# Mirrored tiles of groups 5 and 6 of a graph-attention layer: transposed on TensorE instead of VectorE and DMA, and multiplied in their own step

## The reference

```
h    = relu(layernorm(x)) @ weight                     # 4096 x 256
hn   = h / norm(h)                                     # rows of length 1
P    = exp(hn @ hn.T) * (adj + 1e-8)                   # softmax of sim + log(adj + EPS), before the division
out  = (P @ h) / rowsum(P) + bias
x    = x + out
```

## Time and profile before

| | |
|---|---|
| time, median of 3 runs | 1313.46 us (1306.77 to 1319.57) |
| the profiled execution's own time | 1324.26 us |
| its span | 1322.5 us |
| granted TensorE clock, mean | 0.997 |
| PE busy | 1265.3 us (96%) |
| DVE busy | 986.2 us (75%) |
| ACT busy | 674.7 us (51%) |
| POOL busy | 348.5 us (26%) |

### The profile page before, as it was taken

The page is one execution under the profiler, slowest core; times in us unless marked ns, Lnnn a source line. Parts: engine busy times, 40 slices in busy tenths (PEclk is TensorE's granted clock), DMA queues, the critical chain, the costliest instruction groups (busy, mean ns, idle before and its releaser), DMA issues.

```text
span 1322.5 us, 26821 instructions
## 1 busy us (share of the span) xinstructions
PE 1265.3 (96%) x9548; PEld 942.2 (71%) x9548; DVE 986.2 (75%) x2264; ACT 674.7 (51%) x1504; POOL 348.5 (26%) x423
## 2 busy tenths in 40 slices
PE   6999989988999999989999999999999988989998
PEld 4788878863455555557777777777777766878887
DVE  7968777899555555569899978988989998674352
ACT  6664535555322223256565755766757654635421
POOL 2000000012423222222323322333332322354443
PEclk9999999999999999999999999999999999999999
DMA  9999999951121221025663553553646323351400
GB/s 230 282 291 336 327 325 327 370 216 60 57 65 49 64 65 32 17 64 169 188 186 112 168 176 122 173 174 111 189 133 178 116 96 105 96 160 39 130 26 25
DMA packets 122900, 199.95 MB, mean 151 GB/s; under 512 B 13200, under 2 KB 83856, under 8 KB 122768
## 3 DMA queue, kind: packets, MB, share of 16 engines
q1 hardware_dynamic: 115568, 194.04, 48.0%
q10 hardware_dynamic: 7200, 4.20, 1.1%
HBM read 147.85 MB, written 50.33 MB: 150 GB/s over the span
## 4 chain that ended last, share of the span: by engine, by line
PE 58%; DVE 13%; issue 8%; DMA 5%; POOL 4%; ACT 2%; SPq 1%; ACTq 1%; DVEq 0%; POOLq 0%
PE ps L1797 11%; PE ps L1684 8%; PE ps L1685 8%; PE ps L1782 7%; PE ps L1783 7%; PE ps L1892 7%; DMA acc<-in_adj 5%; DVE ring L834 4%; PE ps L1814 4%; PE ps L1853 3%; DVE small L846 2%; POOL ring L732 1%; SPq L469 1%; POOL w_all L755 1%; ACTq L485 1%
## 5 line engine op out<-in xcount | busy, mean ns | idle before, releaser
L732 POOL TENSOR_TENSOR ring<-ring 128x512 f16<-128x512 f32 (+2 forms) x133 | 148.7, 1119 | 354.0 <-ACT ring L1532 347.0
L1646 PE MATMUL ps<-val_hi,ring 128*128 128x257 f16 x1024 | 227.4, 274 | 8.4 <-DVE ring L834 8.4
L1647 PE MATMUL ps<-val_lo,ring 128*128 128x256 f16 x1024 | 227.3, 274 | 0.0
L1684 PE MATMUL ps<-ring,acc 128*128 128x512 fp8e4 x512 | 195.1, 381 | 8.5 <-DVE acc L972 8.5
L1797 PE MATMUL ps<-hnt 128*128 128x512 f16 (+3 forms) x864 | 196.3, 363 | 0.0
L1685 PE MATMUL ps<-ring,acc 128*128 128x512 fp8e4 x512 | 195.0, 381 | 0.0
L834 DVE STREAM_TRANSPOSE ring<-acc 128x1024 uint8<-128x1024 uint8 x128 | 151.0, 1218 | 40.3 <-DMA acc<-in_adj 40.2
L1411 ACT ACTIVATE hnt<-ring 128x512 bf16<-128x512 uint8 (+1 forms) x192 | 115.1, 602 | 88.1 <-DVE ring L834 88.1
L1782 PE MATMUL ps<-val_hi,hs 128*128 128x257 f16 x534 | 145.8, 273 | 0.4 <-DVE acc L1145 0.3
L1814 PE MATMUL ps<-val_hi,hs 128*128 128x257 f16 x534 | 145.8, 273 | 0.0
L1783 PE MATMUL ps<-val_lo,hs 128*128 128x256 f16 x534 | 145.6, 273 | 0.0
(11 more groups left out here) (234 smaller groups left out, 2384.0 us busy)
## 6 DMA issues: line engine op xcount, KB each, us to landing
acc<-in_adj SPq DMA_DIRECT2D x256, 256.0 KB, 9.1
turned_dram<-ring SPq DMA_DIRECT2D x56, 512.0 KB, 2.9
ring<-turned_dram SPq DMA_DIRECT2D x224, 128.0 KB, 2.9
at_dram<-ring SPq DMA_DIRECT2D x32, 512.0 KB, 10.1
ring<-at_dram SPq DMA_DIRECT2D x64, 256.0 KB, 4.0
ring<-at_dram SPq DMA_DIRECT2D x24, 512.0 KB, 3.9
ring<-at_dram SPq DMA_DIRECT2D x9, 1024.0 KB, 9.8
xs<-in_x SPq DMA_DIRECT2D x12, 256.0 KB, 10.5
```

What stands on the lines that cost most here:

```text
L732: nc.gpsimd.tensor_tensor(lo2[m % 2][:, k:GW], p2t[m % 2][:, k:GW], hi2[m % 2][:, k:GW], ALU.subtract).then_inc(sem["lo2_done"], 1)
L1646: nc.tensor.matmul(ps[:, k % 8, 0:D + 1], lhs, val_hi0[:, t, 0:D + 1], start=(t == 0), stop=False)
L1647: last = nc.tensor.matmul(ps[:, k % 8, 0:D], lhs, val_lo0[:, t, :], start=False, stop=(t == NB - 1))
L1684: nc.tensor.matmul(ps[:, bank + c, :], g_hi[:, t, c * P:(c + 1) * P], src, start=(t == 0), stop=False)
```

## The change

Outer steps of groups 5 and 6 become **near**, those of groups 0 to 4 stay **far**. For a near step the transpose on DVE, the write to DRAM and the read back are gone. PE transposes its four blocks into bank 6 (as for inner steps), DVE masks them in one operation of 128 x 512 out of bank 6, and the mirrored product comes in the step itself and not four steps later. The mirrored product of inner steps of groups 5 and 6 also moves from one step later to the step itself. Near products all go to bank 7, and so do far products at steps in which bank 6 holds transposes. The counts waited for are renumbered (`rank` is the place among outer steps in the order of the mirrored products; `flipped` is inner or near).

```diff
@@ -308,12 +308,17 @@
         n_outer = [sum(outer[:n]) for n in range(NS + 1)]
         n_inner = [sum(inner[:n]) for n in range(NS + 1)]
         LAG = 4
+        NEAR = 5
+        near = [outer[n] and order[n][0] >= NEAR for n in range(NS)]
+        far = [outer[n] and not near[n] for n in range(NS)]
+        flipped = [inner[n] or near[n] for n in range(NS)]
+        n_flipped = [sum(flipped[:n]) for n in range(NS + 1)]
 
         def mirrors_at(n):
 
 
-            return ([n - LAG] if 0 <= n - LAG < NS and outer[n - LAG] else []) + \
-                [o for o in (n - 1, n) if 0 <= o < NS and inner[o] and o + (order[o][0] < NG - 1) == n]
+            return ([n - LAG] if 0 <= n - LAG < NS and far[n - LAG] else []) + \
+                [o for o in (n - 1, n) if 0 <= o < NS and flipped[o] and o + (order[o][0] < NEAR) == n]
 
         mirror_order = [o for n in range(NS + LAG) for o in mirrors_at(n)]
         place = {o: m for m, o in enumerate(mirror_order)}
@@ -326,7 +331,7 @@
             for n in range(NS):
                 if outer[n]:
                     at = n + LAG
-                    free = at > 20 and not any(inner[o] and o - 1 <= at <= o for o in range(NS))
+                    free = far[n] and at > 20 and not any(flipped[o] and o - 1 <= at <= o for o in range(NS))
                     past = banks[n] = 6 if free and past == 7 else 7
             return banks
 
@@ -339,7 +344,14 @@
         def sums_in(bank, n):
 
 
-            return max([n_outer[o] + 1 for o in range(n) if outer[o] and mirror_bank(o) == bank] + [0])
+            return max([rank[o] + 1 for o in rank if rank[o] < rank[n] and mirror_bank(o) == bank] + [0])
+
+        rank = {o: i for i, o in enumerate(o for o in mirror_order if outer[o])}
+
+        def sums_before(n):
+
+
+            return max([rank[o] + 1 for o in rank if far[o] and o + LAG < n - 1 and mirror_bank(o) == 6] + [0])
 
         def first_block(n):
 
@@ -364,7 +376,7 @@
 
         def mirrored_last(g, b):
 
-            return any(inner[n] and order[n] == (g, g * GB + b) and n + (g < NG - 1) >= last_step(g, b) for n in range(NS))
+            return any(inner[n] and order[n] == (g, g * GB + b) and n + (g < NEAR) >= last_step(g, b) for n in range(NS))
 
         def last_step(g, b):
 
@@ -578,7 +590,7 @@
 
             sp.wait_ge(sem["z_piece"], piece_count(7, 3))
             load_raw(sp, 0, "11")
-            outer_steps = [n for n in range(NS) if outer[n]]
+            outer_steps = [n for n in range(NS) if far[n]]
             chunk_at = {last_in(c - 3) + 2: c for c in range(3, len(pairs))}
             mirror_chunk_at = {last_of(c - 3) + LAG + 1: c for c in range(3, len(mirror_pairs))}
             for n in range(NS):
@@ -1102,7 +1114,7 @@
                 m, r, b0 = place[n], order[n][1] % GB, mirror_blocks(n)[0]
                 since(dve, sem["lo2_done"], m - 1)
                 out = p2t[m % 2][:, b0 * P:GW]
-                if outer[n]:
+                if far[n]:
                     c, o = mirror_chunk_of(n), n_outer[n]
                     if r == 0:
                         dve.wait_ge(c2_loaded[c % 3], 16 * (c // 3 + 1))
@@ -1113,10 +1125,19 @@
                                                               chunk2[c % 3][:, q, r * P:(r + 1) * P].rearrange("p (a j) -> p a j", a=4),
                                                               EDGE * ATTN_EPS, came[:, o % 2, q], ALU.add, ALU.mult)
                     last.then_inc(sem["p2_done"], 1)
+                elif near[n]:
+                    c = mirror_chunk_of(n)
+                    if r == 0:
+                        dve.wait_ge(c2_loaded[c % 3], 16 * (c // 3 + 1))
+                    dve.wait_ge(sem["t_done"], n_flipped[n] + 1)
+                    nc.vector.scalar_tensor_tensor(out.rearrange("p (b i) -> p b i", i=P),
+                                                   chunk2[c % 3][:, :, r * P:(r + 1) * P], EDGE * ATTN_EPS,
+                                                   ps[:, 6, :].rearrange("p (b i) -> p b i", i=P),
+                                                   ALU.add, ALU.mult).then_inc(sem["p2_done"], 1)
                 else:
                     c = chunk_of(n)
                     dve.wait_ge(c1_loaded[c % 3], 16 * (c // 3 + 1))
-                    dve.wait_ge(sem["t_done"], n_inner[n] + 1)
+                    dve.wait_ge(sem["t_done"], n_flipped[n] + 1)
                     nc.vector.scalar_tensor_tensor(out.rearrange("p (b i) -> p b i", i=P),
                                                    chunk1[c % 3][:, b0:GB, r * P:(r + 1) * P], EDGE * ATTN_EPS,
                                                    ps[:, 6, b0 * P:GW].rearrange("p (b i) -> p b i", i=P),
@@ -1124,12 +1145,12 @@
 
             def add_mirror(n):
 
-                (g, j), m = order[n], n_outer[n]
+                g, j = order[n]
                 dve.wait_ge(sem["pv2_done"], place[n] + 1)
                 if g == 0:
                     nc.vector.tensor_copy(acc[:, j, :], ps[:, mirror_bank(n), 0:D + 1]).then_inc(sem["acc_added"], 1)
                 else:
-                    dve.wait_ge(sem["acc_added"], m - NB + (g + 1) * GB)
+                    dve.wait_ge(sem["acc_added"], rank[order.index((g - 1, j))] + 1)
                     nc.vector.tensor_tensor(acc[:, j, :], acc[:, j, :], ps[:, mirror_bank(n), 0:D + 1], ALU.add).then_inc(sem["acc_added"], 1)
 
             def group_sum(g, b):
@@ -1141,7 +1162,7 @@
                 if g == 0:
                     nc.vector.tensor_copy(acc[:, k, :], ps[:, b, 0:D + 1]).then_inc(sem["group_out"], 1)
                 else:
-                    dve.wait_ge(sem["acc_added"], n_outer[opens[g]])
+                    dve.wait_ge(sem["acc_added"], max(rank[o] + 1 for o in rank if o < opens[g]))
                     nc.vector.tensor_tensor(acc[:, k, :], acc[:, k, :], ps[:, b, 0:D + 1], ALU.add).then_inc(sem["group_out"], 1)
 
             def group_tail(g, i):
@@ -1310,7 +1331,7 @@
             for n in range(NS):
                 if n + 1 < NS:
                     weights(n + 1)
-                if n + 1 < NS and outer[n + 1]:
+                if n + 1 < NS and far[n + 1]:
                     turn(n + 1)
                 for o in mirrors_at(n - 1):
                     if outer[o]:
@@ -1335,14 +1356,14 @@
                     residual2(late_at["project1"][n])
                 if n + 1 < NS:
                     for o in mirrors_at(n + 1):
-                        if n + 1 in opens and outer[o]:
+                        if n + 1 in opens and far[o]:
                             mirror_weights(o)
                 if n + 1 in opens:
                     for b in range(GB):
                         group_sum(order[n][0], b)
                 if n + 1 < NS:
                     for o in mirrors_at(n + 1):
-                        if n + 1 not in opens or inner[o]:
+                        if n + 1 not in opens or flipped[o]:
                             mirror_weights(o)
                 if n in PREP:
                     prepare(n)
@@ -1511,10 +1532,10 @@
                 k = first_block(n) * P
                 nc.scalar.activation(ps[:, 4 + n % 2, k:GW], ps[:, 4 + n % 2, k:GW], ACT.Exp, scale=1.0 / VSC ** 2).then_inc(sem["exp_raw"], 1)
                 if n >= 2:
-                    if outer[n - 2]:
+                    if far[n - 2]:
                         act.wait_ge(sem["turned"], n_outer[n - 2] + 1)
-                    if inner[n - 2]:
-                        act.wait_ge(sem["t_done"], n_inner[n - 2] + 1)
+                    if flipped[n - 2]:
+                        act.wait_ge(sem["t_done"], n_flipped[n - 2] + 1)
                 act.wait_ge(sem["exp_raw"], n + 1)
                 nc.scalar.activation(e_t[n % 2][:, k:GW], ps[:, 4 + n % 2, k:GW], ACT.Copy, scale=PSC).then_inc(sem["exp_done"], 1)
 
@@ -1827,9 +1848,9 @@
             def mirror(n):
 
                 pe.wait_ge(sem["exp_done"], n + 1)
-                if n_inner[n] > 0:
-                    pe.wait_ge(sem["p2_done"], place[[o for o in range(n) if inner[o]][-1]] + 1)
-                since(pe, sem["acc_added"], sums_in(6, n - 1 - LAG))
+                if n_flipped[n] > 0:
+                    pe.wait_ge(sem["p2_done"], place[[o for o in range(n) if flipped[o]][-1]] + 1)
+                since(pe, sem["acc_added"], sums_before(n))
                 for b in mirror_blocks(n):
                     last = nc.tensor.transpose(ps[:, 6, b * P:(b + 1) * P], e_t[n % 2][:, b * P:(b + 1) * P], ident_f[:, :])
                 last.then_inc(sem["t_done"], 1)
@@ -1843,7 +1864,7 @@
                     if bank == 6:
                         for done in ("relu1", "ht2_low", "val2_ready", "hnt_ready"):
                             pe.wait_ge(sem[done], NB)
-                        past = [o for o in range(n + LAG) if inner[o]]
+                        past = [o for o in range(n + LAG) if flipped[o]]
                         if past:
                             pe.wait_ge(sem["p2_done"], place[past[-1]] + 1)
```

(2 more changed lines are left out.)

## The result

The changed kernel takes 1323.47 us (median of 16 runs, 1315.01 to 1337.6) against 1314.81 us for the kernel before (16 runs, 1306.2 to 1324.63). The ratio is 1.0057, with a 95% interval of 1.003 to 1.0084: about 7.5 us slower, between 4 and 11. Two of the 16 runs of the changed kernel (1335.2 and 1337.6 us) lay over 1.5% above its fastest and are left out of the ratio, which is why it is smaller than that of the medians. The forecast was +3.5 us.

The account below looks back on a forecast made before the run. PE was taken as nearly full, its waits mostly for DVE, with 12.9 us idle from step 120 to L3. +5.7 and -2.2 us gave +3.5, a median of 1317.0 us from 1313.46; range 1307 to 1325.

Parts of the forecast that it names:

- rival 2: Near steps: every near product waits in bank 7 for the add of the one before; +14 us, 1327.5; chance 0.10.
- segment 1: Steps 120 to 135: from 65.0 us before to 70.7 after, +5.7 us.
- segment 2: Step 136 to L3: from 25.9 us before to 23.7 after, -2.2 us, set by chains through DVE.
- The sum's first term: PE work added: 12 near steps with four transposes each, 0.44 us a step, 5.3 us in all.
- Two products in one bank: Steps 122 and 123: second product in bank 7 waits for DVE's add of the first; 2.4 us taken, bounds 1.0 and 3.8.
- the walk: Count through DVE's iteration in step 122, add ending at 6.1 us: stalls of 2.1 us there, 0.7 in 123, 2.8 together.
- Group 6: Opening of group 6 with group_sum, two tails and a slow L1161: 0.8 us of waits allowed, bounds 0 and 2.
- the old waits of 1.2, 3.1 and 1.05 us: Steps 120 to 135: claimed to go, as DVE sheds 0.8 us a step and no far sum uses bank 6 there.
- the wait of 3.36 us: Group 7, before a mirrored product: goes in name only, as the direct product of 142 then waits for the same DVE work.
- Rival 1: Step 120 to L3: chains hold and the filler is not missed; -3 us, 1310.5; chance 0.28.
- Rival 3: L3: DVE finishes its operands earlier, so L3 waits less by what its start is late; 0 us; chance 0.12.
- The sign of being wrong: Near steps 128 to 131 taking over 4.5 us each, or group 7 shortening by over 3 us.

Follow-up runs that it names:

- experiment 5: Changed kernel plus 18 unread matmuls after the inner transposes of steps 135 and 142 each; L2's first scores to L3 549.7 us, changed kernel 551.5.
- experiment 4: Changed kernel with every near transpose issued twice, 48 more; ratio to the kernel before 1.0074 (1.0043 to 1.0106).
- experiment 1: Changed kernel with group 5's four diagonal rows first (order 0, 3, 1, 2); ratio to the kernel before 1.0015 (0.998 to 1.005).
- Experiment 6: Changed kernel with group 5's tail spread over later iterations; L2's first scores to L3 551.5 us, as in the changed kernel.
- experiments 7 and 9: Changed kernel with group 5's diagonal rows first and its tail spread, run once, then timed; ratio to the kernel before 0.9986, 1310.4 us for 1313.2.

## Why the forecast was right, and where it was too small

The forecast was no change within 1%, with a small loss in it, and a range of 1307 to 1325 us. The measured 1323.47 us lies 1.5 us inside its upper end. The sign and the mechanism held; the loss is twice the +3.5 us, and it stayed in the range because that was drawn to take in most of rival 2, which did not happen. That part is luck. I had also taken 1% as what can be told from no change: with 16 runs on each side the interval is 0.5% wide, and the loss is clear of none. Without falls (experiment 5) segment 1 takes 73.6 us and segment 2 24.4, together 98.0 for the 94.4 of the forecast.

**The sum's first term held.** Four transposes cost 0.44 us of PE, 5.3 us in all; the pitch is 0.11 us in the rows, and experiment 4 puts 3.6 us of a second helping on the path. The figure of about 275 ns a transpose that the Trainium skill gives (TensorE: Matmul & The Clock Gate, Part 4: PE-mode transpose) is this trace's duration of one, 273 ns, and not its price. Nor did doubled transposes lower the clock: the mean over the runs of experiment 4 was 0.9972, against 0.9955.

**Two products in one bank: right in place and kind, small in size.** Forecast 2.1 and 0.7 us, taken as 2.4 together; measured 2.49 and 0.86, 3.35 together, and experiment 1 took away 3.7. DVE in iterations 122 and 123, in the timeline of the changed kernel, does what the walk said:

```profile
1029.57 0.68 DVE L1094 SCALAR_TENSOR_TENSOR ring<-ring,ps 128x512 f32<-128x512 fp8e4 x1
...
1031.55 0.89 DVE L1124 SCALAR_TENSOR_TENSOR ring<-ring 128x128 f32<-128x128 fp8e4 x4
1032.36 0.68 DVE L1133 SCALAR_TENSOR_TENSOR ring<-ring,ps 128x512 f32<-128x512 fp8e4 x1
1032.95 0.48 DVE L1182 SCALAR_TENSOR_TENSOR xs<-acc,small,xs 128x256 f32<-128x256 f32 x1
...
1033.90 0.53 DVE L1094 SCALAR_TENSOR_TENSOR ring<-ring,ps 128x384 f32<-128x384 fp8e4 x1
1034.36 0.42 DVE L1154 TENSOR_TENSOR acc<-acc,ps 128x257 f32<-128x257 f32 x1
```

The add at 1034.36 is the one that PE waits for; before it stand the far mask, the near mask, the tail and the weights of 124. I had the walk at 2.8 us and shaded it down on a guess. What the walk itself missed is its start: DVE began iteration 122 at 1029.57, 1.36 us into PE's step (1028.21), where I had taken 1, because L1182 of the iteration before took 1.38 us in place of 0.48.

**Group 6: the step that was mis-sized.** I allowed 0.8 us and wrote that the old waits of 1.2, 3.1 and 1.05 us go. They did, but 2.54 us came before product 134. It is the lateness of DVE that had held transposes of 135 for 3.1 us before, now with another waiter: bank 7 instead of bank 6. Two rows of DVE show it:

```profile
1084.90 1.45 DVE L1182 SCALAR_TENSOR_TENSOR xs<-acc,small,xs 128x256 f32<-128x256 f32 x1
...
1087.67 0.42 DVE L1154 TENSOR_TENSOR acc<-acc,ps 128x257 f32<-128x257 f32 x1
```

L1182, 0.48 us by itself, took 1.45 here, and the one at 1080.21 us took 1.38. A low half on POOL (L744) begins beside each, at 1084.92 and 1080.16 us; I had named the long form and allowed for less than one of them. Experiment 6 shrank the wait to 0.70 by moving tail work alone. With 3.35 for 2.4 and 2.54 for 0.8 this accounts for 2.7 of the 2.8 us by which segment 1, without its fall, exceeds the forecast (75.2 - 1.7 = 73.5, +8.5 for +5.7).

**Segment 2** was forecast as 23.7 and took 24.7, 24.4 in experiment 5 without a fall, so it is 0.7 us too small; waits of 4.7 us in group 7 were foreseen (4 or more). That the wait of 3.36 us would go in name and its time would stay is what the rows show: the direct product of 142 now waits 2.66.

**The clock was left out.** Two falls are in the profile after and none in the profile before. I should have asked whether the one profile of before, with waits of over 3 us and no fall, was typical. By the mean clocks it was not; and so the clock does not explain the medians.

**The rivals.** Rival 1 (idle time falls by more than the transposes cost) is refuted: idle went from 12.9 to 13.2. Rival 2 (every near product late) did not happen: of eight near products of group 5, only those of 122, 123 and one with 0.27 us waited for an add, and of group 6's four only that of 134. The sign of being wrong that belongs to it, steps 128 to 131 of over 4.5 us each, did not come: they take 4.37, 4.80, 4.37 and 4.26 us. Rival 3 is refuted by L3's unchanged 207 us.

## What to carry to other kernels

When an engine waits for another one's queue, relief by removing operations counts only if they stand before the late operation in that queue in the iteration in question; find that iteration, and ask what takes the place of the waiter. An accumulator bank used twice in one step makes a round trip through the other engine's whole iteration, here 2.5 us for an add of 0.4. And with steps written out by hand, compare a stretch between two fixed instructions: where these kernels do the same work it repeats to 0.1 us (451.6 or 451.7 up to step 120 in every profile), while whole runs vary by 1%.

## What was not expected of the hardware

- The fall of the clock is not a function of the wait alone. Waits of 3.1 and 3.4 us were followed by none in one profile; the same wait of 2.49 us by none in three and by a fall in a fourth. Waits of 2.54 to 2.71 us were followed by a fall in nine of ten cases. A fall took 1.7 us of full-rate time, twice or three times that in two cases, and the profiles of this study hold from none to three of them in the stretch, also between two profiles of one and the same kernel (experiments 7 and 9: none and one, after the same wait of 2.66 us).
- With two waits filled with matmuls that nobody reads, both falls were absent, and it cost nothing, as the waits were longer than the filling: 1.8 us shorter with 36 matmuls more. It is one profile, to be read beside the nine falls in ten.
- A DVE operation with both tensors in SBUF (L1182, 128 x 256) took 1.38 to 1.45 us in place of 0.48 three times in groups 5 to 7 of the changed kernel, where POOL's L744 had begun from 0.13 us before to 0.02 us after it, and 0.48 the other nine times. In the same stretch POOL's 16 operations of 512 columns took 1176 ns in the mean, before 1255.
